# Two macaron blocks with 8-expert feed-forward layers on one core: the up-weights of each tile brought to their buffer by a transfer that the sync engine issues, in place of a copy on ScalarE

## What is computed

```
x = x + 0.5 * _L0_ffn_ref(_layernorm(x), ...)    # experts: silu(x Wg) * (x Wu), then Wd, 344 wide
x = x + _L0_attn_ref(_layernorm(x), ...)         # RWKV: a scan over the tokens
x = x + 0.5 * _L0_ffn_ref(_layernorm(x), ...)
x = x + 0.5 * _L1_ffn_ref(_layernorm(x), ...)    # experts: silu(x we1 + be1), then we2, 512 wide
x = x + _L1_attn_ref(_layernorm(x), ...)         # retention, 16 heads of 8
x = x + 0.5 * _L1_ffn_ref(_layernorm(x), ...)
```

## Time and profile before

| | |
|---|---|
| median of 3 runs | 757.58 us (757.11 to 758.16) |
| profiled execution, its own time | 756.79 us |
| its span | 755.0 us |
| mean granted clock of TensorE | 0.932 of full speed |
| busy: PE, PEld, DVE, ACT, POOL | 611.3, 514.5, 420.4, 346.6, 395.7 us |
| moved by DMA | 50.28 MB, mean 67 GB/s |

### The profile page before, as it was taken

The page is one execution under the profiler, slowest core; times in us unless marked ns, Lnnn a source line. Parts: engine busy times, 40 slices in busy tenths (PEclk is TensorE's granted clock), DMA queues, the critical chain, the costliest instruction groups (busy, mean ns, idle before and its releaser), DMA issues.

```text
span 755.0 us, 13385 instructions
## 1 busy us (share of the span) xinstructions
PE 611.3 (81%) x4216; PEld 514.5 (68%) x4248; DVE 420.4 (56%) x1156; ACT 346.6 (46%) x661; POOL 395.7 (52%) x405
## 2 busy tenths in 40 slices
PE   1288996978478798898989879998678699988792
PEld 0288996757356797798879867664623279977782
DVE  6726225797849964654146054859899876232002
ACT  1154863763248464574775545231111234755351
POOL 3176787561577346767776774321000466267742
PEclk9998998999699998998999999999789699999897
DMA  8166213201322011332231231002000112114213
GB/s 344 33 196 195 57 39 100 43 16 43 89 53 34 15 56 52 97 80 43 79 108 41 53 107 36 22 12 69 1 11 17 26 40 46 49 44 135 51 33 101
DMA packets 42977, 50.28 MB, mean 67 GB/s; under 512 B 8352, under 2 KB 34336, under 8 KB 42912
## 3 DMA queue, kind: packets, MB, share of 16 engines
q0 software_dynamic: 11776, 24.14, 13.2%
q1 hardware_dynamic: 31136, 25.28, 10.3%
HBM read 32.09 MB, written 17.30 MB: 65 GB/s over the span
## 4 chain that ended last, share of the span: by engine, by line
PE 49%; DVE 17%; POOL 13%; issue 9%; DMA 8%; ACT 2%; SPq 1%; ACTq 0%; DVEq 0%; POOLq 0%
PE bank L587 12%; PE bank L565 9%; PE bank L574 8%; POOL xs L1020 7%; DMA xs<-tokens_in,idx_in 6%; PE bank L663 5%; POOL tokens_out L1030 4%; PE bank L691 4%; PE bank L546 2%; PE bank L511 2%; DVE mixer L1305 2%; PE bank L491 1%; PE bank L572 1%; DMA yg<-tokens_out 1%; DVE hT L1210 1%
## 5 line engine op out<-in xcount | busy, mean ns | idle before, releaser
L1030 POOL DMA_INDIRECT tokens_out<-ys,idx_out x184 | 189.9, 1032 | 179.8 <-ACT ys L850 140.3
L1020 POOL DMA_INDIRECT xs<-tokens_in,idx_in x184 | 180.1, 979 | 156.9 <-DVE owner L1190 80.3
L788 ACT ACTIVATE w_up<-w 128x728 f32 (+1 forms) x184 | 131.2, 718 | 136.6 <-PE bank L565 66.5
L587 PE MATMUL bank<-w,hT 128*128 x1288 | 181.5, 284 | 8.4 <-ACT ys L850 3.0
L587 PEld LDWEIGHTS bank<-w,hT 128*128 128x128 f32 x1288 | 163.4, 196 | 24.0 <-issue 22.6
L565 PE MATMUL bank<-xT_kept,w_up 128*128 128x128 f32 x1104 | 159.2, 296 | 8.3 <-DVE hT L1210 5.0
L565 PEld LDWEIGHTS bank<-xT_kept,w_up 128*128 128x128 f32 x1104 | 147.8, 209 | 16.5 <-DVE hT L1210 7.5
L1210 DVE TENSOR_TENSOR hT<-gate,bank 128x384 f32<-128x384 f32 x92 | 50.7, 551 | 101.6 <-PE bank L565 72.5
L1226 DVE SCALAR_TENSOR_TENSOR x<-yg,cw,x 128x128 f32<-128x128 f32 x128 | 37.4, 340 | 125.1 <-DMA yg<-tokens_out 125.0
L574 PEld LDWEIGHTS bank<-xT_kept,w_up 128*128 128x128 f32 x736 | 97.7, 193 | 7.4 <-issue 4.6
L574 PE MATMUL bank<-xT_kept,w_up 128*128 128x128 f32 x736 | 97.7, 276 | 6.1 <-issue 2.1
(11 more groups left out here) (166 smaller groups left out, 674.6 us busy)
## 6 DMA issues: line engine op xcount, KB each, us to landing
yg<-tokens_out SPq DMA_DIRECT2D x64, 128.0 KB, 2.7
w<-in_w SPq DMA_DIRECT2D x8, 536.0 KB, 9.6
tokens_in<-xn SPq DMA_DIRECT2D x16, 256.0 KB, 2.6
w<-in_w SPq DMA_DIRECT2D x8, 512.0 KB, 9.4
xs<-tokens_in,idx_in POOLq DMA_INDIRECT x184, 2.6
tokens_out<-ys,idx_out POOLq DMA_INDIRECT x184, 2.3
x<-in_x SPq DMA_DIRECT2D x2, 512.0 KB, 8.6
out<-x SPq DMA_DIRECT2D x8, 128.0 KB
```

The lines of the kernel that those rows point to most:

```text
L587: last = mm(y, hT[0:n_f, n % 2, c * P:(c + 1) * P], w_of(k, e, WD[k] + c * P, P, n_f), start=(c == 0), stop=(k == 0 and c == CH[k] - 1))
L788: nc.scalar.activation(w_up[:, n % 3, 0:UP[k]], w_of(k, e, 0, UP[k]), ACT.Copy).then_inc(w_copied, 1)
L1020: pool.indirect_dma_start(xs[:, j % RING, :], None, xn_dram[b], tile_rows(idx_in, b, j))\
L1030: pool.indirect_dma_start(ys_dram[b], tile_rows(idx_out, b, j), ys[:, j % RING, :], None)\
```

## The change

ACT no longer copies the up-weights. SP gets a sixth generator, `up_weights` (letter f), which for each of the 184 tiles waits for its buffer, loads the owner from `te` into a register, and issues a transfer from SBUF to SBUF (128 partitions of 2912 bytes for kind 0, 2048 bytes for kind 1). PE waits for that transfer's own semaphore, one for each of the three buffers. ACT's generator `copies_w` and its registers go.

```
-        w_copied = sem("w_copied")
+        ld_w_up = [sem(f"ld_w_up{i}") for i in range(3)]
...
+            def up_weights():
+                for p, (f, b) in enumerate(PASSES):
+                    for j in range(TILES):
+                        yield
+                        if j == 0:
+                            sp.wait_ge(RT_DVE[b].sem, RT_DVE[b].done(SUB[f], "te"))
+                            if f in (0, 3) and b == 0:
+                                sp.wait_ge(ld_w[KIND[f]], 16 * E)
+                        k, n = KIND[f], p * TILES + j
+                        if n >= 3:
+                            sp.wait_ge(up_ready, up_made(n - 3, 1))
+                        sp.reg_load(owners[j % len(owners)], te[0:1, b * NSB + j:b * NSB + j + 1])
+                        e = sp.snap(owners[j % len(owners)], min_val=0, max_val=E - 1)
+                        sp.dma_start(w_up[:, n % 3, 0:UP[k]], w_of(k, e, 0, UP[k])).then_inc(ld_w_up[n % 3], 16)
...
-                pe.wait_ge(w_copied, n + 1)
+                pe.wait_ge(ld_w_up[n % 3], 16 * (n // 3 + 1))
...
-                nc.scalar.activation(w_up[:, n % 3, 0:UP[k]], w_of(k, e, 0, UP[k]), ACT.Copy).then_inc(w_copied, 1)
```

`TURNS` is written anew for all five engines. Of SP's, the start:

```
-        "b e a3 b2 c7 d a6 b6 a6 c b6 a4 b4 a2 b2 a4 d4 b4 e4",
+        "a c7 b e f d a2 f3 b2 f26 a2 f a2 f16 a2 b4 f20 b2 f8 a4 f8 a2 f14 c f b4 f6 b2 f18 a f a2 f a f15 b4 a2 f19 "
```

More of the change, by code:

```diff
@@ L426, in rows @@
                                          by_token(ys_dram[b], s * S)[:, 2 * i:2 * i + 2, :]).then_inc(ld_yg[b][i], 16)
+            owners = [sp.alloc_register(f"sp_owner{i}") for i in range(4)]
+            def up_weights():
[12 more added lines that the diff above has]
+                        sp.dma_start(w_up[:, n % 3, 0:UP[k]], w_of(k, e, 0, UP[k])).then_inc(ld_w_up[n % 3], 16)
             def later_loads():
@@ L461, in _ @@
             sp.dma_start(x[:, NT:2 * NT, :], x_in[:, NT:2 * NT, :]).then_inc(ld_x[1], 16)
-            weave(TURNS["sp"], rows(0), rows(1), later_loads(), results(0), results(1))
+            weave(TURNS["sp"], rows(0), rows(1), later_loads(), results(0), results(1), up_weights())
             sp.wait_ge(st_out, 16 * NB * NT // 2)
@@ L745, in run @@
                 nc.scalar.activation(dst, src, func, **kw).then_inc(steps.sem, 1)
-            owners = [act.alloc_register(f"act_owner{i}") for i in range(4)]
-            def load_owner(b, j):
-                act.reg_load(owners[j % len(owners)], te[0:1, b * NSB + j:b * NSB + j + 1])
             def norm(f, b):
@@ L779, in route @@
                 run(gap[:, b, 1, :], gap[:, b, 0, :], ACT.Tanh, RT_ACT[b], scale=0.5)
[L781 to L785, removed]
-                load_owner(PASSES[p][1], j)
-                e = act.snap(owners[j % len(owners)], min_val=0, max_val=E - 1)
-                nc.scalar.activation(w_up[:, n % 3, 0:UP[k]], w_of(k, e, 0, UP[k]), ACT.Copy).then_inc(w_copied, 1)
             def copies_x():
@@ L851, in copies_y @@
                             .then_inc(y_copied, 1)
-            def copies_w():
-                for p, (f, b) in enumerate(PASSES):
-                    for j in range(TILES):
-                        yield
-                        if j == 0:
-                            after(RT_DVE[b], SUB[f], "te")
-                            if f in (0, 3) and b == 0:
-                                act.wait_ge(ld_w[KIND[f]], 16 * E)
-                        copy_w(p, j)
             def silus():
@@ L923, in _ @@
             nc.scalar.activation(rw_v[:, 3:4], colv[:, DECAY:DECAY + 1], ACT.Exp).then_inc(RW_EXP.sem, 1)
-            weave(TURNS["act"], silus(), beside(0), beside(1), copies_w(), copies_x(), copies_y(), rwkv_weights(), retention_tables())
+            weave(TURNS["act"], silus(), beside(0), beside(1), copies_x(), copies_y(), rwkv_weights(), retention_tables())
         @block.gpsimd
```

## The result

The changed kernel takes **772.6 us** (median of 4 runs, 771.4 to 774.3), the kernel before 757.4 beside it: ratio **1.0215**, interval 1.0172 to 1.0259. A second measurement gave 1.0238 (1.0211 to 1.0265). It is 15 to 18 us slower where the prediction said 8 us faster, and it lies outside the predicted range of 735 to 768.

The account below looks back on a forecast made before the run. PE, POOL and, in the mixers, DVE were taken to bound the kernel in turns. The sum 756.8 - 2 + 5 - 2.7 - 5 - 3 = 749.1, plus 0.8, gave 750 us, range 735 to 768.

Parts of the forecast that it names:

- contention: Gathers meeting weight transfers on the 16 DMA engines: 20 landings, each 0.25 us later, 5 us lost.
- 2 of copies: Taking the copies out of ACT's queue frees activations queued behind them: 2 us gained.
- Order, start: Start and pass 0, w1 and sq loaded right behind w0: fewer gather waits, scatters of pass 0 earlier, 2.7 us gained.
- Order, pass 2: Boundary of pass 2: yg loads early, 2.5 us, and first RWKV product of b 1 earlier, 3 us; together 5 gained.
- the gain of the two late gathers: Two chain gathers of 5.73 and 8.20 us fall to about 2.6: 8.7 us less waiting.
- The step's formula: Last scatter of pass 0, POOL's 60th transfer: 34.9 + 59 x 1.26 = 109.2, with 1 us of waits 110.2.
- a start held by w1 past 37 us: Named among the signs that would prove the prediction wrong: early w1 loads delaying the start beyond 37 us.
- Order, end: Passes 6 and 7: pass 7 starts 11 us later, last phase 14 us shorter, net 3 us gained.
- ring of three: Three up-weight buffers: a tile every (latency + 1.5)/3 us, above PE's 2.0 only beyond 4.5 us latency.
- weights late: Slower rival: SP's queue brings weights after PE's turn; 15 us lost, 764 us, chance 0.1.
- The transfer's price: Each up-weight transfer on SP: 0.47 us to issue, 3.0 us to land for kind 0.
- SP's in-order queue: Transfers held behind SP's scatter waits and yg loads: counted as nothing, up to 3 us once a pass for the range.

Follow-up runs that it names:

- run 3: The kernel before, ACT still copying the up-weights, under the changed kernel's order on all five engines: 768.6 us, ratio 1.0141.
- run 4: The kernel before with sq, the biases and the w1 loads early, ahead of the first store of tokens_in on SP: 756.3 us, ratio 0.9984.
- old head: Old order through pass 0's first 8 tiles and b 1's route: ratio 1.0117 against the kernel before with copies under the new order, 1.0172 on the changed kernel.
- run 1: The changed kernel with the eight w1 loads spread between the up-weight transfers of tiles 13 to 20: 775.9 us, ratio 1.0233 against the kernel before.
- run 7: The kernel before with the changed kernel's order after pass 5 on PE, ACT, DVE and POOL: 759.3 us, ratio 1.0020.
- small transfers: Transfers under the old order, each from the fourth on cut to 128 columns: 760.6 us, ratio 1.0036 against the kernel before.

## Why the prediction was wrong

**The sign is lost in the order, the rest in a size.** The prediction summed 10.7 us gained from the order (2.7 + 5 + 3) and 3 lost to the mechanism (5 of contention less 2 of copies). With the order alone the runs lose 10.7 us (12.2 by the medians, and part of it may be the placing of the copies, run 3), and the mechanism adds about 6.

**The failed steps: "Order, start" and "Order, pass 2".** Together they were to gain 7.7 us by the first gather of pass 2. With copies the new order is 10.2 us late there (211.6 for 201.4 with w1 early; 10.8 against the kernel before).

*"Order, start"* is the larger miss: 2.7 us gained were forecast, and the loads of `yg` of pass 0 start 8.1 us late (122.1 for 113.9; 6.9 against the kernel before). That w1 ahead of the stores costs at most 3 us was right (2.0, run 4), and so was the gain of the two late gathers: with w1 early the last scatter of pass 0 has 0.8 us of waits where it had 4 (36.4 + 55 x 1.26 + 5.2 is 110.9, and it left at 111.6). What failed is that only SP's and POOL's queues were read there. DVE's new order has the first row table 4.0 us later, so the first gather left at 39.0 for 34.9. PE's has the transposes and the route of b 1 ahead of the first gathered tile, which was transposed at 48.2. The step's formula gives 39.0 + 59 x 1.26 = 113.4 for the last scatter; it ran at 119.6, with 6.3 us of waits in place of the 1 taken, 5.3 of them for PE's transposes. With the old head, and copies, there are 5.5 us between this order and the old one (117.1 for 111.6), about the four extra transfers that the prediction had counted, 5.0; it had set against them the bias preparation, which that head has among the scatters again. The prediction named "a start held by w1 past 37 us" as what would prove it wrong: the start was held past 37, but not by w1 (run 1).

*"Order, pass 2"* priced two things that come earlier, the loads of `yg` (2.5) and the first RWKV product of b 1 (3). The first came: from the route's first step on DVE to the gather the new order takes 12.1 us with copies, the old one 14.4. For the second it fits that the lateness shrinks to 6.0 us by the first gather of pass 3 (297.1 for 291.1; 8.5 against the kernel before). What the step put at nothing is the price of the same 46 products, where 43.5 were, in the stretch ahead of the route. From the first add of `yg` to the route's first step that stretch takes 74.5 us in the new order with copies (124.9 to 199.4), for 70.3 with w1 early (116.7 to 187.0) and 68.3 before (118.1 to 186.4): 4.2 to 6.2 us more. Two and a half more tiles at 2.0 us are 5 us of PE. That this is the cause is read from the profile; no kernel moved these products alone. The empty window of the route is no cause of that lateness, since the gather follows the route sooner than before.

**A place not spoken of: pass 5.** Between the first gathers of passes 4 and 5 the new order with copies loses 7 us more (7.6 to 14.7 against w1 early, 9.1 to 16.0 against the kernel before). DVE has the owners `te` of pass 5 10.9 us late (420.4 for 409.5). At that place POOL has 16 scatters of pass 4 ahead of the first gather of pass 5, before it had 14, and it waited up to 3.3 us for `ys` between them (2.6 with w1 early).

**"Order, end": the mechanism right, the size too good.** On its own (run 7, new tail) pass 6 starts at 571.2 where 573 was estimated, and pass 7 at 675.0 where 673 was. The last phase from there took 68.7 us where 65 to 66 were. The net is 1.5 us lost for 3 gained, within the bounds given (12 gained to 9 lost). In the full new order the tail takes up a part of the lateness of pass 5: 4 us against w1 early (14.7 to 10.7), 1.1 against the kernel before (16.0 to 14.9). Where that room comes from was not followed.

**What each place is worth in the median is open.** The head is worth 1.8 us with copies (by the ratios; 3.9 by each kernel's median against its own kernel before) and, with w1 moved as well, 4.8 in the changed kernel (771.1 for 775.9); the tail loses 1.5. The rest of the 10.7 us, some 4 to 7, lies from the second half of pass 0 to pass 5, where no kernel changed one place alone.

**Contention, right in this order and mis-sized beside bulk loads.** 20 landings with 0.25 us each made 5 us, all on gathers. Measured: 5.6 to 7.3 us in the new order (a difference of two kernels), 15 us by bytes under the old one. The sum was built on the transfer's mean share (18% of the time) and left out that two large ones meet: with w1 beside them transfers of weights took 5.5 to 6.1 us, over the 4.5 us that the prediction's ring of three allows. So the rival "weights late" had the right symptom, 18.3 us of PE's waits for `w_up`; 7.1 of them went with the bytes, and the others stayed. In the new order, though, the same meeting cost nothing that lasted (run 1: 1.0233, with the loads of `yg` 4.0 us later). The rule of the Trainium skill, "DMA: Bandwidth & Descriptors", section "Issuing engines are not separate DMA queues", that transfers of all issuers share 16 engines, is what the trace shows here: under the old order most slices from 87 to 105 us stand at 380 to 430 GB/s, and gathers (5.6 us at the median from 80 to 120 us, 2.6 before) and weights both land late.

**What held.** The transfer's price (0.49 us to issue, 2.8 us to land). The estimate of 2.9 us from the Trainium skill, "DMA: Bandwidth & Descriptors", section "Anatomy of one DMA", agrees with it, though the page fits its figures to transfers that GpSimd issues. PE's direct wait in the new order (5.1 us for "under 5"), and no large cost of SP's in-order queue (2.7 us in all with small transfers, which also bounds what ACT's lost copies gave back: no gain of them shows). The other signs missed: the first load of `yg` (122.0 for 112 to 114), and the gathers of pass 6 (584.4 for 570 to 576) and of pass 7 (687.8 for 665 to 675). ACT was busy 238.7 us and not 215: the profile counts overlapping instructions once. Before, ACT's groups add up to 375.2 us for 346.6 of busy time, now to 245.3 for 238.7, so taking the copies' 131.2 off 346.6 took off too much. PE's busy time did not fall to 605 but rose from 611.3 to 615.3; what makes up these 4 us was not followed.

## What to carry to other kernels

Work that an engine does without delaying anyone gave nothing here when it was taken away, and on the DMA engines it competed with transfers that others wait for: price the bytes where they meet other bulk loads too, not only by their mean share. Where an order is rewritten, ask for each boundary not only what comes earlier but what now has to run ahead of it, and read every engine's order there, PE's and DVE's as well as the queues. A rewritten order and a changed mechanism are two changes: measured apart they were 1.4% and 2.4%, together 2.2 to 2.4%.

## What was not expected of the hardware

Two of five chips needed 867 and 876 us for the kernel that the others ran in 756 to 758. With small transfers PE's weight load stood still behind "issue" there for 63.5 us at one line, up to 6.3 us at once, where the same kernel and line have 18.2 and at most 1.2 us on a chip of 758 us. The mean granted clock was lower too, 0.88 and 0.89 for 0.93, and PE was busy 656.6 and 649.9 us for 612.0. Of full transfers and a changed order with the old head (1.7% on a chip of 758 us) 0.0 and 0.4% were left there: a comparison can vanish on another chip, and the time of the kernel before, on the same chip, is what shows that it is another. Why these chips are so is open.
